# A fused LayerNorm, linear attention and MLP kernel: two of its four batches normalised with channels on the partitions

## The chip, the cores and the metric

The kernel runs on one core of a Trainium2 chip. The metric is the time of one execution on the device in microseconds (us); a kernel's time is the median of its runs. The engines are TensorE (PE; its weight loads are PEld), VectorE (DVE), ScalarE (ACT), GpSimd (POOL) and SyncE (SP), which here issues every DMA, in the order of its program.

## The reference

`x` has 4 batches of 512 tokens and 512 channels, in float32. Scales, shapes and names are shortened:

```python
xn = (x - mean(x)) / sqrt(var(x) + 1e-5)            # over the channels
q, k, v = xn @ wq.T, xn @ wk.T, xn @ wv.T           # 16 heads of 128; k and v have 4
o = lightning_attn(rope(q), rope(k), v)             # causal, decay exp(-lam_h * (i - j))
s = o @ wo.T
f = silu(xn @ fp8(gate_w) * gate_scale) * (xn @ fp8(up_w) * up_scale)   # 1536 wide
g = silu(f @ fp8(down_w) * down_scale)
out = x + s * g
```

## The kernel before

`xn` is used with channels on the partitions. Each product's operands are kept in two parts, a rounded one ("hi", a cast to fp32r by ScalarE) and the rest ("lo", a subtraction by VectorE or GpSimd). P = 128, KT = TT = 4 (channel tiles and token tiles), MT = 12 tiles of the hidden dimension. Batches are taken in `ORDER = [1, 2, 3, 0]`, and `s` is the position in it, so `s` = 2 and 3 are the third and fourth batch taken. A LayerNorm tile `i` is tile `i % 4` of batch `i // 4`.

*LayerNorm.* `load_x(i)` (L292) brings a tile of 128 tokens, tokens on the partitions, into one of 6 slots of `stage`. VectorE takes its statistics (`tile_stats`, `mean_var`, `inv_std`; the power runs on GpSimd). For `s` = 0 and 1 VectorE normalises, for `s` = 2 and 3 ScalarE (`norm`, L505). TensorE turns the tile with four transposes of 128x128 (`ln_transpose`, L1333) into a PSUM bank, ScalarE casts it to `xn`'s high part (`norm_hi`, L510), VectorE writes the rest (`norm_lo`, L809). Transposes of `s` = 2 and 3 all use bank 7.

*First loop (L1397), `m` = 0 to 11.* TensorE runs `gate_up` for `s` = 0 and 1 (each a gate and an up product chain of 8 matmuls), then `down(m - 2)` of `s` = 0; the engines beside it round the weights to fp8 values (`w_exponent`, `w_floor`, `w_round`). The tiles of `s` = 2 are turned at `m` = 7 to 10.

*Second loop (L1406), steps (`s`, `m`) with `s` = 2, then 3.* A step is `gate_up(s, m)`, for `m` < 4 a tile of `v` (`v_tile`, bank 7), then `down` of the batch before it. `gate_up` has three banks: `silu_gate(m)` (ScalarE) frees the gate's, which the up chain of `m` + 1 takes, and `fuse(m)` (VectorE) the up's, which the gate chain of `m` + 2 takes. `fuse_hi` (ScalarE) and `fuse_rest` (GpSimd) split `f` for `down`. At (2, 4) to (2, 7) the tiles of `s` = 3 are turned. In each step from (2, 1) to (3, 4) half a tile of `v` is multiplied by decay (`vd_mult`, VectorE), cast (`vd_round`, ScalarE), subtracted (`vd_rest`, VectorE) and stored as `v_decayed` (`store_vd`, SP); it has two buffers, so `vd_round` waits for the stores of the step before:

```python
if y >= 2:
    act.wait_ge(vd_out[y % 2], 16 * (y // 2))
```

At (3, 0) ScalarE makes the gates of `s` = 1 (`gates`, L546), for which TensorE waits before its first `down` of `s` = 2; ScalarE's `v_round` and VectorE's `v_rest` free bank 7 for the next `v_tile`. `spill_xn` and `spill_last` store `xn` (2 MB each batch, for `s` = 3 in four parts from (2, 8) on), and the first `attn_w` (1.28 MB) is loaded into `stage` at (2, 8).

*Attention.* After the second loop, 16 steps (head group, batch) follow, with `transpose_k` (L1440) in each. The change doesn't touch them.

The order on each engine is that of the program; engines meet through the semaphores named in the code.

## Time and profile before

| what | value |
|---|---|
| median of 3 runs | 905.67 us (905.59 to 906.05) |
| profiled execution, its time | 905.21 us |
| its span, first to last instruction | 903.4 us |
| TensorE busy | 895.4 us, 99% |
| VectorE busy | 632.6 us, 70% |
| ScalarE busy | 418.6 us, 46% |
| GpSimd busy | 373.4 us, 41% |
| DMA | 138.55 MB, mean 153 GB/s |

The span lies 1.8 us inside the time of its execution. The first loop ends near 147 us, the second near 312 us; the attention takes the rest. Busy shares are means over stages with different limits; busy time of TensorE is counted from the start of a matmul to its modelled end, so matmuls that follow one another overlap, and what one costs is read from the distance between starts.

### The profile page before, as it was taken

Reading aid. Unit: us, or ns where it says so; the run is one execution under the profiler, and the core shown is the slowest. Engines: PE = TensorE matmul, PEld = TensorE weight load, DVE = VectorE, ACT = ScalarE, POOL = GpSimd, SP = SyncE. Lnnn points to the kernel's source line nnn. Section 1 sums busy time; section 2 is a strip of 40 time slices with the busy share of each in tenths; the row PEclk is TensorE's granted clock in tenths of the full one; section 3 lists DMA queues with packets and bytes.
Section 4 is the critical chain, followed back from the end, with each engine's and each line's share of the span. In section 5 each row is a group of like instructions: output and inputs, shape, how many; then the busy total and the mean of one; then the engine's idle time right before and its main releaser. Section 6 shows DMA issues by size and latency. Waiting matters only on the chain.

```text
span 903.4 us, 12444 instructions
## 1 busy us (share of the span) xinstructions
PE 895.4 (99%) x4122; PEld 739.6 (82%) x4122; DVE 632.6 (70%) x905; ACT 418.6 (46%) x705; POOL 373.4 (41%) x276
## 2 busy tenths in 40 slices
PE   8999999999999999999999999999999999999997
PEld 5878888888888888888888888888888888888886
DVE  7978653677653257766777867677767677788797
ACT  3443533443433456444455444463554554634542
POOL 1011112122122475536555456365454563553547
PEclk9999999999999999999999999999999999999999
DMA  6792304379760624413333513244243043264482
GB/s 213 212 398 89 105 24 152 143 254 322 276 223 6 210 94 161 153 43 144 140 117 141 190 55 140 69 181 169 81 163 131 32 178 145 95 234 147 165 259 82
DMA packets 51115, 138.55 MB, mean 153 GB/s; under 512 B 4224, under 2 KB 25344, under 8 KB 45696
## 3 DMA queue, kind: packets, MB, share of 16 engines
q1 hardware_dynamic: 51072, 138.00, 43.2%
q8 instruction: 24, 0.39, 0.2%
q14 instruction: 19, 0.16, 0.1%
HBM read 96.04 MB, written 41.94 MB: 153 GB/s over the span
## 4 chain that ended last, share of the span: by engine, by line
PE 86%; issue 6%; POOL 4%; DVE 3%; ACT 1%; DMA 0%; POOLq 0%; SPq 0%; DVEq 0%; ACTq 0%
PE bank L1274 85%; POOL d_r L1210 2%; POOL rot L1219 1%; PE bank L1332 1%; PE bank L1294 0%; DMA stage<-in_x_nat 0%; DVE tail_sb L1116 0%; PE bank L1448 0%; DVE wst L834 0%; DVE d_sb L1019 0%; DVE tail_sb L1118 0%; ACT mag L522 0%; DVE tail_sb L1102 0%; DVE fz L851 0%; DVE acc L1112 0%
## 5 line engine op out<-in xcount | busy, mean ns | idle before, releaser
L1274 PE MATMUL bank<-xn,aw 128*128 128x512 f32 x960 | 229.1, 390 | 0.0
L1219 POOL TENSOR_TENSOR rot<-rot 128x512 f32<-128x512 f32 x80 | 126.9, 1586 | 234.9 <-DVE rot L1006 234.9
L1274 PEld LDWEIGHTS bank<-xn,aw 128*128 128x128 f32 x960 | 179.0, 188 | 37.3 <-issue 0.7
L1274 PE MATMUL bank<-o_r,ow 128*128 128x512 f32 (+1 forms) x792 | 186.2, 385 | 0.0
L1210 POOL TENSOR_TENSOR d_r<-d_sb,d_r 128x512 fp32r<-128x512 f32 x127 | 166.9, 1339 | 37.2 <-ACT d_r L692 37.1
L1274 PE MATMUL bank<-xn,gu_w 128*128 128x512 f32 x768 | 180.0, 389 | 0.4 <-DVE fz L851 0.4
L1274 PEld LDWEIGHTS bank<-xn,gu_w 128*128 128x128 f32 x768 | 144.1, 188 | 30.9 <-DVE dn_w L843 0.8
L1274 PEld LDWEIGHTS bank<-o_r,ow 128*128 128x128 f32 x792 | 144.4, 188 | 28.5
L1005 DVE TENSOR_TENSOR rot<-bank,rope 128x512 f32<-128x512 f32 x80 | 55.2, 690 | 102.6 <-ACT rot L672 102.5
L671 ACT COPY rot<-bank 64x512 f32<-64x512 f32 x80 | 46.8, 585 | 154.6 <-PE bank L1274 154.2
L692 ACT CAST d_r<-d_sb 128x512 fp32r<-128x512 f32 x128 | 79.0, 621 | 84.6 <-DVE d_sb L1065 62.2
L1191 POOL TENSOR_TENSOR fsplit<-f_all,fsplit 128x512 fp32r<-128x512 f32 x36 | 48.0, 1339 | 130.3 <-ACT fsplit L544 130.3
L1274 PE MATMUL bank<-fsplit,dn_w 128*128 128x512 f32 x384 | 94.7, 392 | 0.0
L1019 DVE TENSOR_TENSOR d_sb<-rot,q_decay 128x256 f32<-128x256 f32 x64 | 88.8, 1405 | 1.2 <-POOL rot L1219 1.2
L1274 PEld LDWEIGHTS bank<-fsplit,dn_w 128*128 128x128 f32 x384 | 71.3, 188 | 14.9 <-issue 0.3
L1065 DVE TENSOR_TENSOR d_sb<-bank,decay 128x512 f32<-128x512 f32 x96 | 64.2, 686 | 22.0 <-PE bank L1274 20.6
L1274 PE MATMUL bank<-q_r,k_r 128*128 128x512 f32 x288 | 78.2, 391 | 0.0
L1274 PE MATMUL bank<-d_r,v_r 128*128 128x512 f32 (+1 forms) x336 | 76.8, 361 | 0.4 <-POOL d_r L1210 0.4
L1274 PEld LDWEIGHTS bank<-d_r,v_r 128*128 128x128 f32 x336 | 57.5, 188 | 13.1 <-POOL d_r L1210 2.0
L1274 PEld LDWEIGHTS bank<-q_r,k_r 128*128 128x128 f32 x288 | 53.1, 188 | 10.3
L851 DVE SCALAR_TENSOR_TENSOR f_all<-bank,scale_sb,f_all 128x512 f32<-128x512 f32 x36 | 26.9, 748 | 47.0 <-PE bank L1274 36.7
L1191 POOL TENSOR_TENSOR fsplit<-fz,fsplit 128x512 fp32r<-128x512 f32 x12 | 15.5, 1294 | 103.3 <-ACT fsplit L544 103.3
(87 smaller groups left out, 973.4 us busy)
## 6 DMA issues: line engine op xcount, KB each, us to landing
xn<-xn_split SPq DMA_DIRECT2D x15, 2048.0 KB, 7.8
v_decayed<-vd_split SPq DMA_DIRECT2D x32, 512.0 KB, 3.5
vd_r<-v_decayed SPq DMA_DIRECT2D x16, 1024.0 KB, 7.2
v_r<-v_split SPq DMA_DIRECT2D x16, 512.0 KB, 5.8
wst<-in_mlp_w SPq DMA_DIRECT2D x10, 768.0 KB, 5.2
xn_split<-xn SPq DMA_DIRECT2D x3, 2048.0 KB, 10.7
stage<-in_attn_w SPq DMA_DIRECT2D x4, 1280.0 KB, 5.7
stage<-in_x_nat SPq DMA_DIRECT2D x16, 256.0 KB, 5.0
```

Source lines behind the costliest of these rows:

```text
L671: act.copy(rot2[0:ROT, r % RRING, :], ps[ROT:, :])
L692: act.copy(d_r[:, slot(e), 0, :], d_sb[:, slot(e), :]).then_inc(d_hi, 1)
L851: dve.scalar_tensor_tensor(out=f, in0=gu_ps[(2 * u + 1) % 3][:], scalar=scale_sb[:, MT + m:MT + m + 1], in1=f, op0=ALU.mult, op1=ALU.mult) ...
L1005: dve.tensor_tensor(rot1[:, r % RRING, :], proj_bank(n, r)[:], rope[:, 0, :], ALU.mult)
L1019: dve.tensor_tensor(d_sb[:, slot(e), bass.ts(h % 2, HALF)], rot1[:, (h + 1) % RRING, HALF:S], q_decay[:, h, :], ALU.mult).then_inc(q_decay ...
L1065: dve.tensor_tensor(by_head(d_sb[:, slot(e), :]), by_head(sc_ps[t % TRING][:]), decay[:, h0:h0 + nh, i0 - j:i0 - j + ni, :], ALU.mult).the ...
L1191: pool.tensor_tensor(fsplit[:, e % FRING, 1, :], src, fsplit[:, e % FRING, 0, :].bitcast(F32), ALU.subtract).then_inc(f_lo, 1)
L1210: pool.tensor_tensor(d_r[:, slot(e), 1, :], d_sb[:, slot(e), :], d_r[:, slot(e), 0, :].bitcast(F32), ALU.subtract).then_inc(d_lo, 1)
L1219: pool.tensor_tensor(rot1[:, r % RRING, :], rot1[:, r % RRING, :], rot2[:, r % RRING, :], ALU.add).then_inc(qk_sum, 1)
L1274: last = pe.matmul(dst, a, b, start=start and x == 0, stop=stop and x == len(pairs) - 1)
L1332: last = pe.transpose(ln_ps(i)[:, bass.ts(k, P)], stage[:, i % XRING, bass.ts(k, P)], ident[:])
```

## The change

For `s` = 0 and 1 nothing changes. For `s` = 2 and 3, x is still loaded with tokens on the partitions, for its statistics alone. Mean and rstd of the batch (128 partitions, 4 + 4 columns) are copied side by side into `row_in_sb`, turned by one transpose (`turn_rows`) into 8 partitions of 128, copied to `row_sb` (`row_round`), stored to DRAM (`store_rows`), and loaded from there as two rows of 512 tokens, each spread over all 128 partitions (`load_rows`), into the first half of `gout`. x is loaded again with channels on the partitions (`load_xt`, from `x_t`, which the kernel already has as an input). VectorE subtracts the one row and multiplies by the other (`norm_t`); ScalarE casts (`norm_t_hi`), VectorE writes the rest (`norm_t_lo`). The transposes of `ln_transpose` for tiles 8 to 15, ScalarE's `norm` and the `norm_hi` and `norm_lo` of those tiles are gone.

The places move: `norm_t` of `s` = 2 stands at `m` = 10 and 11 of the first loop, that of `s` = 3 at (2, 7) and (2, 8). `spill_last` and the load of `attn_w` go from (2, 8) to (2, 10) and on. The diff, without its declarations of semaphores and its blank lines:

```diff
 SPILL = 4
-LND = 4
+SPILL_AT = [(2, 10), (2, 11), (3, 0), (3, 1)]
+NAT = [i % XRING for i in range(3 * TT)] + [4, 5, 0, 1]
+TURNED = {2: [0, 1, 2, 3], 3: [2, 3, 4, 5]}
...
         xn_dram = nc.dram_tensor("xn_split", (NB, P, 2, KT, S), F32, kind="Internal").ap()
+        row_dram = nc.dram_tensor("ln_rows", (2, 2 * TT, P), F32, kind="Internal").ap()
...
         rstd = sb("rstd", [P, NB * TT], scope=mlp)
-        nmr = sb("nmr", [P, NB * TT], scope=mlp)
+        row_in_sb = sb("row_in_sb", [P, 2 * TT], scope=mlp)
+        row_sb = sb("row_sb", [2 * TT, P], scope=mlp)
         mlp.close()
+        rows = gout[:, 0:2, :]
...
...
-            return bank[i % TT] if i < 2 * TT else bank[7]
+            return bank[i % TT]
...
             def load_x(i):
-                if i >= XRING:
+                if i >= 3 * TT + 2:
+                    sp.wait_ge(ln_lo, 2 * TT + NAT[i] + 1)
+                elif i >= 3 * TT:
+                    sp.wait_ge(stats_d, i - 1)
+                elif i >= XRING:
                     sp.wait_ge(ln_t, i - XRING + 1)
-                sp.dma_start(stage[:, i % XRING, :], x_nat[ORDER[i // TT], :, i % TT, :]).then_inc(x_in[i % XRING], 16)
+                sp.dma_start(stage[:, NAT[i], :], x_nat[ORDER[i // TT], :, i % TT, :]).then_inc(x_in[NAT[i]], 16)
+            def store_rows(s):
+                sp.wait_ge(row_d, s - 1)
+                sp.dma_start(row_dram[s - 2], row_sb[:]).then_inc(row_out, 16)
+            def load_xt(s, k):
+                if s == 2:
+                    sp.wait_ge(ln_t if k < 2 else stats_d, 2 * TT if k < 2 else 2 * TT + k - 1)
+                else:
+                    sp.wait_ge(ln_lo if k < 2 else stats_d, 2 * TT + k + 3 if k < 2 else 3 * TT + k - 1)
+                sp.dma_start(stage[:, TURNED[s][k], :], x_t[k, :, bass.ts(ORDER[s], S)]).then_inc(xt_in[k], 16)
+            def load_rows(s):
+                if s == 2:
+                    for r in range(2):
+                        sp.wait_ge(v_out[r], 32 * (2 * TT // VFIRST))
+                else:
+                    sp.wait_ge(gate_out, 16 * KT)
+                sp.wait_ge(row_out, 16 * (s - 1))
+                for r in range(2):
+                    row = row_dram[s - 2, r * TT:(r + 1) * TT].rearrange("t p -> (t p)")
+                    sp.dma_start(rows[:, r, :], row.unsqueeze(0).broadcast_to([P, S])).then_inc(row_in, 16)
...
                 load_w(m)
+            store_rows(2)
+            for k in range(KT):
+                load_xt(2, k)
+            load_rows(2)
...
                         store_vd(*VD_AT[s, m])
+                    if s == 2 and m == 4:
+                        store_rows(3)
+                    if s == 2 and 2 <= m < 2 + KT:
+                        load_xt(3, m - 2)
+                    if s == 2 and m == 5:
+                        load_rows(3)
...
                         fetch_v((m + 1) // 2)
-                    if s == 2 and m >= MT - SPILL:
-                        spill_last(m - (MT - SPILL))
-                    if (s, m) == (2, MT - SPILL):
-                        sp.wait_ge(ln_t, NB * TT)
+                    if (s, m) in SPILL_AT:
+                        spill_last(SPILL_AT.index((s, m)))
+                    if (s, m) == SPILL_AT[0]:
+                        sp.wait_ge(ln_lo, NB * TT)
...
         def _(act):
-            def norm(i):
-                act.wait_ge(rstd_d, i // TT + 2)
-                act.activation(stage[:, i % XRING, :], stage[:, i % XRING, :], ACT.Identity,
-                               bias=nmr[:, i:i + 1], scale=rstd[:, i:i + 1]).then_inc(normed, 1)
...
                 act.wait_ge(ln_t, i + 1)
-                if i == 3 * TT:
-                    act.wait_ge(xn_out0, 16)
...
                          ln_ps(i)[:].rearrange("p (k c) -> p k c", k=KT)).then_inc(ln_hi, 1)
+            def row_round(s):
+                act.wait_ge(row_t, s - 1)
+                if s > 2:
+                    act.wait_ge(row_out, 16 * (s - 2))
+                act.copy(row_sb[:], bank[7][0:2 * TT, 0:P]).then_inc(row_d, 1)
+            def norm_t_hi(s, k):
+                act.wait_ge(scaled, (s - 2) * KT + k + 1)
+                if s == 3 and k == 0:
+                    act.wait_ge(xn_out0, 16)
+                    act.wait_ge(gu_done, 2 * UNIT[1, MT - 1] + 2)
+                act.copy(xn_of(s)[:, 0, k, :], stage[:, TURNED[s][k], :]).then_inc(ln_hi, 1)
...
                     w_floor(PARTS * SLABS + m + 2 - SLABS)
-                if m in (6, 7):
-                    norm(2 * TT + 2 * (m - 6))
-                    norm(2 * TT + 2 * (m - 6) + 1)
-                if 7 <= m < 7 + TT:
-                    norm_hi(2 * TT + m - 7)
+                if m == 7:
+                    row_round(2)
+                if m in (MT - 2, MT - 1):
+                    norm_t_hi(2, 2 * (m - MT + 2))
+                    norm_t_hi(2, 2 * (m - MT + 2) + 1)
...
                         v_round(VT_AT[s, m])
-                    if s == 2 and m in (2, 3):
-                        norm(3 * TT + 2 * (m - 2))
-                        norm(3 * TT + 2 * (m - 2) + 1)
-                    if s == 2 and LND <= m < LND + TT:
-                        norm_hi(3 * TT + m - LND)
+                    if s == 2 and m == 4:
+                        row_round(3)
+                    if s == 2 and m in (7, 8):
+                        norm_t_hi(3, 2 * (m - 7))
+                        norm_t_hi(3, 2 * (m - 7) + 1)
...
             def tile_stats(i):
-                dve.wait_ge(x_in[i % XRING], 16 * (i // XRING + 1))
-                dve.bn_stats(stats[:, i, :], stage[:, i % XRING, :]).then_inc(stats_d, 1)
+                dve.wait_ge(x_in[NAT[i]], 16 * (NAT[:i].count(NAT[i]) + 1))
+                dve.bn_stats(stats[:, i, :], stage[:, NAT[i], :]).then_inc(stats_d, 1)
...
                 dve.wait_ge(newton, c + 3)
-                dve.scalar_tensor_tensor(out=nmr[:, i0:i1], in0=mv[:, i0:i1, 0], scalar=-1.0, in1=rstd[:, i0:i1],
-                                         op0=ALU.mult, op1=ALU.mult).then_inc(rstd_d, 1)
+                if grp > 3:
+                    dve.wait_ge(row_t, grp - 3)
+                dve.tensor_copy(row_in_sb[:, 0:TT], mv[:, i0:i1, 0]).then_inc(row_src, 1)
+                dve.tensor_copy(row_in_sb[:, TT:2 * TT], rstd[:, i0:i1]).then_inc(row_src, 1)
...
                 dve.tensor_tensor(lo, ln_ps(i)[:].rearrange("p (k c) -> p k c", k=KT), hi.bitcast(F32),
+                                  ALU.subtract).then_inc(ln_lo, 1)
+            def norm_t(s, ks):
+                dve.wait_ge(row_in, 32 * (s - 1))
+                c = (s - 2) * KT
+                for k in ks:
+                    dve.wait_ge(xt_in[k], 16 * (s - 1))
+                    xt = stage[:, TURNED[s][k], :]
+                    dve.tensor_tensor(xt, xt, rows[:, 0, :], ALU.subtract).then_inc(centred, 1)
+                for k in ks:
+                    dve.wait_ge(centred, c + k + 1)
+                    xt = stage[:, TURNED[s][k], :]
+                    dve.tensor_tensor(xt, xt, rows[:, 1, :], ALU.mult).then_inc(scaled, 1)
+            def norm_t_lo(s, k):
+                dve.wait_ge(ln_hi, s * TT + k + 1)
+                dve.tensor_tensor(xn_of(s)[:, 1, k, :], stage[:, TURNED[s][k], :], xn_of(s)[:, 0, k, :].bitcast(F32),
...
                     inv_std(3)
-                if 7 <= m < 7 + TT:
-                    norm_lo(2 * TT + m - 7)
+                if m in (MT - 2, MT - 1):
+                    norm_t(2, (2 * (m - MT + 2), 2 * (m - MT + 2) + 1))
+                if m == MT - 1:
+                    norm_t_lo(2, 0)
+                    norm_t_lo(2, 1)
                 fuse(1, m)
+            norm_t_lo(2, 2)
+            norm_t_lo(2, 3)
...
                         v_rest(VT_AT[s, m])
-                    if s == 2 and LND <= m < LND + TT:
-                        norm_lo(3 * TT + m - LND)
+                    if s == 2 and m in (7, 8):
+                        norm_t(3, (2 * (m - 7), 2 * (m - 7) + 1))
+                    if s == 2 and m in (8, 9):
+                        norm_t_lo(3, 2 * (m - 8))
+                        norm_t_lo(3, 2 * (m - 8) + 1)
...
                     pe.wait_ge(ln_lo, v + TT)
+                    pe.wait_ge(v_lo, v)
...
                     pe.wait_ge(ln_lo, i - TT + 1)
-                elif i in (2 * TT, 3 * TT):
-                    pe.wait_ge(v_lo, i)
-                elif i > 2 * TT:
-                    pe.wait_ge(ln_lo, i)
...
                 last.then_inc(ln_t, 1)
+            def turn_rows(s):
+                pe.wait_ge(row_src, 2 * (s - 1))
+                pe.wait_ge(v_lo, TT if s == 2 else 3 * TT)
+                pe.transpose(bank[7][0:2 * TT, 0:P], row_in_sb[:], ident[:]).then_inc(row_t, 1)
...
                 gate_up(UNIT[1, m])
-                if 7 <= m < 7 + TT:
-                    ln_transpose(2 * TT + m - 7)
+                if m == 7:
+                    turn_rows(2)
...
                         v_tile(VT_AT[s, m])
-                    if s == 2 and LND <= m < LND + TT:
-                        ln_transpose(3 * TT + m - LND)
+                    if s == 2 and m == 4:
+                        turn_rows(3)
```

## Rows read from the trace of the kernel before

**Rows 1.** Page, parts 1 and 2: busy time, and the granted clock in 40 slices.
```profile
PE 895.4 (99%) x4122; PEld 739.6 (82%) x4122; DVE 632.6 (70%) x905; ACT 418.6 (46%) x705; POOL 373.4 (41%) x276
...
PEclk9999999999999999999999999999999999999999
```

**Rows 2.** Busy time by stretch: PE, PEld, DVE, ACT, POOL (instructions), clock, DMA share, GB/s.
```profile
60.00:147.00 87.00, 87.00 (x393) 71.97 (x392) 55.55 (x68) 34.10 (x44) 13.93 (x11) 1.00 0.30 115
147.00:312.00 165.00, 165.00 (x736) 136.38 (x735) 92.17 (x129) 72.06 (x122) 38.74 (x30) 1.00 0.58 205
```

**Rows 3.** Timeline, TensorE: start us, us from first start to last end, instructions.
```profile
94.38 1.98 PE L1274 MATMUL bank<-fsplit,dn_w 128*128 128x512 f32 x8
96.19 7.42 PE L1274 MATMUL bank<-xn,gu_w 128*128 128x512 f32 x32
103.45 0.60 PE L1332 MATMUL bank<-ident,stage 128*128 128x128 f32 x4
...
105.74 7.43 PE L1274 MATMUL bank<-xn,gu_w 128*128 128x512 f32 x32
...
183.40 0.60 PE L1332 MATMUL bank<-ident,stage 128*128 128x128 f32 x4
...
185.70 3.80 PE L1274 MATMUL bank<-xn,gu_w 128*128 128x512 f32 x16
```

**Rows 4.** Timeline, TensorE, first step of the attention part.
```profile
356.82 0.38 PE L1448 MATMUL bank<-ident,rot 128*128 128x128 f32 x2
...
359.79 2.88 PE L1274 MATMUL bank<-xn,aw 128*128 128x512 f32 x12
362.51 2.88 PE L1274 MATMUL bank<-o_r,ow 128*128 128x512 f32 x12
365.23 2.88 PE L1274 MATMUL bank<-xn,aw 128*128 128x512 f32 x12
```

**Rows 5.** Groups by line and form, 60 to 330 us: busy us, mean ns, idle before.
```profile
L886 DVE TENSOR_TENSOR vd_split<-vd_sb,vd_split 128x512 fp32r<-128x512 f32 x32 | 21.6, 688 | 21.9 <-ACT vd_split L582 21.6
L544 ACT CAST fsplit<-f_all 128x512 fp32r<-128x512 f32 x34 | 21.1, 622 | 6.7 <-PE bank L1274 6.6
...
L507 ACT ACTIVATE stage<-stage,nmr,rstd 128x512 f32<-128x512 f32 x8 | 6.1, 807 | 0.0
...
L813 DVE TENSOR_TENSOR xn<-bank,xn 128x512 fp32r<-128x512 f32 x8 | 5.5, 687 | 13.3 <-ACT xn L515 13.3
...
L515 ACT CAST xn<-bank 128x512 fp32r<-128x512 f32 x8 | 4.7, 581 | 1.7 <-PE bank L1332 1.6
```

**Rows 6.** Tile `v_decayed`, 150 to 260 us: landing times of its stores.
```profile
DMA to landing us min/median/max: 2.6/3.6/8.1
```

**Rows 7.** Timeline, VectorE (first row) and TensorE.
```profile
138.27 0.75 DVE L851 SCALAR_TENSOR_TENSOR fz<-bank,scale_sb,fz 128x512 f32<-128x512 f32 x1 [3.52 <-PE bank L1274]
...
147.13 3.79 PE L1274 MATMUL bank<-xn,gu_w 128*128 128x512 f32 x16
...
197.57 3.80 PE L1274 MATMUL bank<-xn,gu_w 128*128 128x512 f32 x16
...
225.28 3.79 PE L1274 MATMUL bank<-xn,gu_w 128*128 128x512 f32 x16
228.91 2.88 PE L1274 MATMUL bank<-wv,xn 128*128 128x512 f32 x12
231.63 1.98 PE L1274 MATMUL bank<-fsplit,dn_w 128*128 128x512 f32 x8
```

**Rows 8.** Timeline, GpSimd (first row) and VectorE.
```profile
188.42 1.30 POOL L1191 TENSOR_TENSOR fsplit<-f_all,fsplit 128x512 fp32r<-128x512 f32 x1 [6.38 <-ACT fsplit L544]
...
188.58 1.69 DVE L872 TENSOR_TENSOR v_raw<-vs 128x512 f32<-128x512 f32 x1
...
203.16 1.28 DVE L886 TENSOR_TENSOR vd_split<-vd_sb,vd_split 128x512 fp32r<-128x512 f32 x2
```

**Rows 9.** Timeline, ScalarE, the gates of the batch `s` = 1.
```profile
228.64 2.42 ACT L551 ACTIVATE gout<-bank,scale_sb 128x512 f32<-128x512 f32 x4
```

More of the change, by code:

```diff
@@ L228, in attention_mlp_kernel @@
         floor_c = sem("floor_c"); newton = sem("newton"); rstd_d = sem("rstd_d")
+        row_src = sem("row_src"); row_t = sem("row_t"); row_d = sem("row_d"); row_out = sem("row_out"); row_in = sem("row_in"); xt_in = [sem(f"xt_in{k}") for k in range(KT)]; centred = sem("centred"); scaled = sem("scaled")
         normed = sem("normed"); ln_t = sem("ln_t"); ln_hi = sem("ln_hi"); ln_lo = sem("ln_lo")
```

## The prediction

> **What bounds the kernel now.** I read the page first: what is busy, and at what clock. TensorE is busy 99% of the span and the granted clock is in its highest tenth in every slice, the level of 2.4 GHz [rows 1]. Then the busy time by stretch, for the two stretches that the change touches: from 60 to 147 us (`s` = 0 and 1 side by side) and from 147 to 312 us (`s` = 2 and then 3) TensorE is busy for all of both, and VectorE for 64% and 56% [rows 2]. So nobody makes TensorE wait there: each instruction that it no longer executes shortens the kernel by its pitch, unless another engine then comes late. Last I read the timelines: TensorE's for the pitch, VectorE's, ScalarE's and the queue's for how late they already are.
>
> **What is removed.** 32 transposes in 8 groups of 4, each after a `gate_up` and before a `down`. A profile's duration of a pipelined matmul is not its price; the distance between starts is. Without a group, the 8 products of `down` take from 94.38 to 96.19, 1.81 us. With a group, the distance from the transposes to the next `gate_up` is 105.74 - 103.45 = 2.29 us, and in the later stage 185.70 - 183.40 = 2.30 us [rows 3]. So a group costs 0.48 to 0.49 us, and 8 cost 3.9 us.
>
> The Trainium skill (TensorE: Matmul & The Clock Gate, section "Part 4: PE-mode transpose") gives about 275 ns for a transpose in a kernel's context. By that the 32 would be worth 8.8 us, an estimate. A transpose of four lasts 0.27 us in this trace too (0.60 us for four that start 0.12 us apart), but I go by the starts.
>
> **What is added on TensorE.** Two transposes of `row_in_sb` (128x8). The nearest row is the pair in `transpose_k`: with it, 12 products take 359.79 - 356.82 = 2.97 us, without it 365.23 - 362.51 = 2.72 us [rows 4], so 0.12 us each if it is linear, 0.25 us each if the pair's price is all fixed, and nothing at best. I take 0.12, the price per piece that the groups of four show too (0.49 / 4): 0.25 us for both, bounds 0 and 0.5.
>
> Net: 905.21 - 3.9 + 0.25 = 901.56 us for the profiled execution. Its time is 0.46 us below the median of the runs, 905.67; against that median the sum is 902.0.
>
> **What moves to other engines.** ScalarE loses 8 normalisations of 0.80 us and 8 casts of 0.58 us, and gets 8 casts of 0.62 us and two tiny ones: it gains time. VectorE loses 8 subtractions from PSUM of 0.69 us, and gets 24 operations on SBUF of 0.69 us, one every 0.60 us (the pair at 203.16 takes 1.28) [rows 5, 8]: about 9.6 us more in all. In total VectorE's idle time covers that [rows 2]. What decides is where it stands. The queue gets 8 loads of `x_t` (256 KB each), 4 spread rows of 256 KB and 2 tiny stores: some 3 MB.
>
> *The batch `s` = 2, prepared at `m` = 10, 11 of the first loop.* The row path starts at `turn_rows(2)` after `gate_up(1, 7)`, near 103.5 us; even with a store and a load at 8.1 us each, the longest landing of stores of `v_decayed` [rows 6], the rows are there by about 121, and `norm_t` runs only after `fuse(0, 10)`, at 129. Behind those waits on SP stand only loads of x. The hand-over to `gate_up(2, 0)`: `fuse(0, 11)` began at 138.27 [rows 7]; 0.67 for it, 2.4 for four passes, 1.2 for two subtractions, 0.67 for `fuse(1, 11)`, 1.3 for the last two: 144.6, or 145.9 if the GpSimd subtraction stands in the way once (1.3 us). `gate_up(2, 0)` started at 147.13 [rows 7]; all of this shifts together. Covered by 1.2 to 2.5 us, so costed at nothing; with the cover gone, `gate_up(2, 0)` waits for the difference. `spill_xn(2)` (2 MB) now waits for these last subtractions; behind it on SP stand the stores of the gates, which wait for `down(11)` anyway. The x tiles 14 and 15 wait for the first two `norm_t_lo` and are read at (2, 1), more than a unit later.
>
> *GpSimd in the way.* When `v_raw` was added at 188.58, with GpSimd's subtraction running from 188.42, it took 1.69 us [rows 8], where a subtraction of the same shape takes 0.69 [rows 5]. Each of the new passes has two SBUF operands too, so each can be held for up to 1.3 us; `norm_lo` read PSUM. The Trainium skill (SBUF — State Buffer, section "SBUF: two separate sides") says that VectorE with two SBUF inputs and GpSimd exclude each other for a whole instruction; the trace agrees, 1.69 against 0.69 us. It is the rule that speaks against this change. I count one collision below, where ScalarE's release of GpSimd falls on VectorE's start.
>
> *The batch `s` = 3, prepared at (2, 7) to (2, 9), which is `gate_up`'s (`s`, `m`).* Here VectorE is already full: `vd_mult`, `fuse`, `vd_rest`. I write it out from the start of `gate_up(2, 7)` (197.57 before) as 0. A unit is 3.63 + 1.81 = 5.44 us [rows 3, 7], so the starts are 5.44, 10.88, 16.3, 21.8, and 27.2 for (3, 0).
> - (2, 7): the last `vd_rest` ends at 6.9, as before (203.16 + 1.28) [rows 8]. Two centrings, two scalings: 9.3. ScalarE waits for them and casts to 9.9.
> - (2, 8): ScalarE's `fuse_hi` and `silu_gate` end at 11.1; `up(2, 9)` needs them at 12.7. VectorE: `fuse` 11.8, `vd_rest` 13.0, `norm_t` 15.5, two `norm_t_lo` 16.7.
> - (2, 9): ScalarE's gate is done at 17.3, needed at 18.1. VectorE's `v_raw` collides with GpSimd, 18.6; products 19.8, `fuse` 20.5, needed at 21.8; `vd_rest` 21.7, the last two `norm_t_lo` 22.9.
> - (2, 10), (2, 11): `vd_round` waits for the stores of `v_decayed` before it (landing 2.6 to 8.1, median 3.6 us [rows 6]). With 3.0 us it is done with (2, 11) at 30.8, with 3.6 us at 31.9. Then the four gates, 2.42 us [rows 9]: 33.2 to 34.3. `down(3, 0)` needs them at 27.2 + 3.63 + 2.72 = 33.55. Before, they ended at 228.64 + 2.42 = 231.06 and were needed at 231.63 [rows 7, 9]: the margin was 0.57 us already. So 0 to 0.75 us of stall.
> - (3, 0): ScalarE's `vd_round` waits for stores issued at 31.0 to 31.8, now behind `spill_last` and the 1.28 MB of `attn_w` (moved from `m` = 8 to `m` = 10). `v_round(12)` and `v_rest(12)` stand behind it, and `v_tile(13)` wants the bank at 27.2 + 8.16 + 3.63 = 39.0. With a landing of 3.6 us the bank is free by about 37.8 to 38.4, with 5.2 us at 39.6, with 8.1 at 42.5: 0 to 3.5 us.
>
> For the two places together I take 0.5 us, nearer the lower end, as the median landing is 3.6; bounds 0 and 4.2. ScalarE's gain at `m` = 2 to 7 speaks for the lower end. The other new waits (`row_out` at `load_rows(3)`, behind which on SP stand the stores of `m` = 6; `turn_rows(3)` on `v_lo`, which the first transpose of `s` = 3 waited for before too) are met units ahead: nothing.
>
> **Forecast:** 902.0 + 0.5 = 902.5 us, faster by 0.35%.
>
> **Rivals.**
> - *A. The slack at (2, 10) to (3, 1) is gone:* a stall of 1.8 to 5.4 us that eats half to all and more of the gain, time 903.9 to 907.5, likeliest near 904.5. For it: margins of 0.8, 1.3 and 0.57 us, and the landing of 8.1 us. Against it: the transfers that made that landing leave `m` = 8.
> - *B. Slower:* one mechanism, stores of `v_decayed` late behind the spill and `attn_w` at (2, 11), so `v_tile(13)` waits for its bank. Above 907.5 it needs a stall of 5.5 us, so a landing of 10 to 11 us after an issue at 31.8: longer than any landing in that row. Say 12 us: 46.4 - 39.0 = 7.4 us, 909.4.
> - *C. TensorE's transposes were worth nothing or much more.* Worth nothing would be 905.9; TensorE has no idle time in which they could hide [rows 2]. Worth their duration of 0.27 us instead of 0.12, the time would be near 897; the starts speak against it [rows 3].
>
> **How the numbers follow.** A measurement of this kernel tells about 0.2%, 1.8 us, from no change. The forecast with a stall of 0 to 1.8 us has 0.70; A 0.17 within the bound and 0.01 of it beyond; B 0.08; C 0.02 for the nothing and 0.02 for the much. Faster: 0.72. Same: 0.19. Slower: 0.09. The forecast's own range is 901.5 (added transposes free, 0.25 us for noise) to 903.8. The range of 8 in 10 takes in A to 905.5, where under 0.2 is left out on top and below: 901.3 to 905.5.
>
> **What would show it.** Between `down(e)`'s first product and the next `gate_up`, 1.81 us everywhere but after the two `turn_rows` (about 1.95). TensorE still without idle time to (2, 11); if it stalls, at `down(3, 0)` for a gate, at `v_tile(13)` for `v_lo`, or at `up(2, 10)`. VectorE's passes at 0.69 us, some near 1.7. ScalarE idle some 2.5 us at (2, 7) before its casts. Wrong, if the row transposes cost more than 0.3 us, if the spread loads of one DRAM row land after 10 us or more, which no row shows, or if the landing of the stores at (2, 10) doubles.

## The result, and the profile after

The changed kernel takes 908.63 us (median of 8 runs, 907.91 to 910.32) against 905.64 us (8 runs, 905.46 to 906.38): the ratio is 1.0034, 95% interval 1.0025 to 1.0043. It is slower by 3.0 us, where 902.5 us was forecast.

In the profiled execution (span 906.7 us, against 903.4) TensorE executes less, and is busy less, as against [rows 1]:

```profile
PE 892.9 (98%) x4092; PEld 737.1 (81%) x4092; DVE 646.1 (71%) x923; ACT 413.6 (46%) x699; POOL 374.3 (41%) x276
```

The waits of TensorE, in the changed kernel (us in total, times, longest):

```profile
PE bank L1411 <- DVE stage L861: 2.4, 1, 2.4
PE bank L1356 <- ACT gout L604: 1.5, 1, 1.5
PE bank L1356 <- ACT f_all L588: 1.5, 2, 1.0
...
PE bank L1356 <- DVE vs L935: 1.3, 1, 1.3
```

Before, TensorE was busy for all of the stretch from 147 to 312 us [rows 2]. Now it waits there four times for the banks of `gate_up` (1.03 and 0.48 us), for the gates (1.53) and for the bank of `v_tile` (1.32). The timeline of TensorE shows where, and what each really costs:

```profile
182.80 0.27 PE L1418 MATMUL bank<-ident,row_in_sb 128*8 128x128 f32 x1
182.83 2.09 PE L1356 MATMUL bank<-fsplit,dn_w 128*128 128x512 f32 x8
...
206.51 1.98 PE L1356 MATMUL bank<-xn,gu_w 128*128 128x512 f32 x8
209.52 2.11 PE L1356 MATMUL bank<-xn,gu_w 128*128 128x512 f32 x8 [1.03 <-ACT f_all L588]
211.47 1.98 PE L1356 MATMUL bank<-fsplit,dn_w 128*128 128x512 f32 x8
213.28 1.98 PE L1356 MATMUL bank<-xn,gu_w 128*128 128x512 f32 x8
215.74 2.11 PE L1356 MATMUL bank<-xn,gu_w 128*128 128x512 f32 x8 [0.48 <-ACT f_all L588]
217.69 1.98 PE L1356 MATMUL bank<-fsplit,dn_w 128*128 128x512 f32 x8
...
228.57 2.88 PE L1356 MATMUL bank<-wv,xn 128*128 128x512 f32 x12
232.98 2.08 PE L1356 MATMUL bank<-fsplit,dn_w 128*128 128x512 f32 x8 [1.53 <-ACT gout L604]
234.90 3.79 PE L1356 MATMUL bank<-xn,gu_w 128*128 128x512 f32 x16
240.00 3.06 PE L1356 MATMUL bank<-wv,xn 128*128 128x512 f32 x12 [1.32 <-DVE vs L935]
242.90 1.98 PE L1356 MATMUL bank<-fsplit,dn_w 128*128 128x512 f32 x8
```

Read the distances between starts, as in [rows 3, 7]. A transpose of the rows costs 182.80 to 184.75, the start of the next `gate_up`, less 1.81: 0.14 us. The first loop, from the same `down` at 95.62 (94.38 before) to `gate_up(2, 0)` at 146.53 (147.13), is 1.84 us shorter than before, which is what four groups less and one small transpose more should give. Then `gate_up(2, 9)` (from 206.51) takes 4.96 us for 3.63, `gate_up(2, 10)` (from 213.28) 4.41 for 3.63, `v_tile(12)` with its wait 4.41 for 2.72, `gate_up(3, 1)` with the wait behind it 5.10 for 3.63; with the slower restarts (0.11 and 0.18) that is 5.6 us lost, some 0.3 us more at each place than the wait itself. Gained and lost: -3.9 + 0.3 + 5.6 = +2.0 us of the 3.3 by which the spans differ.

The first two of these stalls come from `silu_gate(2, 8)` and `silu_gate(2, 9)`, each of which frees the bank that the up chain of the next step takes. The expectations below name the stalls after these gates, (2, 8) and (2, 9); TensorE stands in `gate_up` of (2, 9) and (2, 10).

Nearly all of the rest is at the start. The stretches of the page's window view at 8 to 12 us (PE, PEld, DVE, ACT, POOL, clock, DMA share, GB/s) show the clock at its lower level, after TensorE had stood idle for 2.36 us before its first transpose:

```profile
8.00:10.00 2.00, 1.26 (x6) 1.29 (x7) 1.89 (x7) 0.76 (x2) 0.00 (x0) 0.60 1.04 376
10.00:12.00 2.00, 2.00 (x9) 1.10 (x7) 1.54 (x6) 2.00 (x5) 0.70 (x1) 0.55 0.63 234
```

That is 1.2 us by `down` at 95.62; the first transpose itself starts 0.57 us late (8.74 for 8.17), and the rest follows at the lower clock. The code there is unchanged, and later profiles of kernels with the change had the same place within 0.5 us of before, so it belongs to this execution. The medians differ by 3.0 us all the same, so that other executions lose about 1 us at some place that this profile doesn't show.

### The profile page after: what moved, and what is told of

It is laid out like the page before. It is cut to its first block, busy times and chain, and to the rows that moved or that the text cites. A ratio compares the mean times of both kernels' runs of the same rounds, so it can differ in the third digit from the quotient of the medians.

```text
span 906.7 us, 12414 instructions
## 1 busy us (share of the span) xinstructions
PE 892.9 (98%) x4092; PEld 737.1 (81%) x4092; DVE 646.1 (71%) x923; ACT 413.6 (46%) x699; POOL 374.3 (41%) x276
## 4 chain that ended last, share of the span: by engine, by line
PE 79%; issue 6%; DVE 5%; POOL 4%; DMA 3%; ACT 1%; SPq 1%; POOLq 0%; DVEq 0%; ACTq 0%
PE bank L1356 78%; POOL d_r L1292 2%; DMA v_decayed<-vd_split 2%; POOL rot L1301 1%; DMA vs<-v_split 1%; DVE vd_split L960 1%; DMA stage<-in_x_nat 0%; PE bank L1376 0%; DVE tail_sb L1198 0%; PE bank L1533 0%; DVE wst L908 0%; DVE d_sb L1101 0%; DVE tail_sb L1200 0%; PE bank L1411 0%; DVE f_all L925 0%
## 5 line engine op out<-in xcount | busy, mean ns | idle before, releaser
L713 ACT CAST q_r<-rot 128x512 fp32r<-128x512 f32 x64 | 39.8, 622 | 39.2 <-POOL rot L1301 38.4
```

The costliest lines, as they stand in the source:

```text
L713: act.copy(dst, rot1[:, r % RRING, :]).then_inc(qk_hi, 1)
```

## Why TensorE waits: the transfers first

SyncE's timeline at (2, 5) and VectorE's at (2, 7), changed kernel:

```profile
192.67 0.46 SPq L318 DMA_DIRECT2D stage<-in_x_t  x1
193.23 1.16 SPq L330 DMA_DIRECT2D gout<-ln_rows  x2
194.43 0.98 SPq L379 DMA_DIRECT2D vs<-v_split  x2
195.67 9.99 SPq L386 DMA_DIRECT2D v_decayed<-vd_split  x4
...
201.41 0.69 DVE L946 TENSOR_TENSOR v_raw<-vs 128x512 f32<-128x512 f32 x1 [4.58 <-DMA vs<-v_split]
...
205.22 1.28 DVE L878 TENSOR_TENSOR stage<-stage,gout 128x512 f32<-128x512 f32 x2
...
195.63 3.79 PE L1356 MATMUL bank<-xn,gu_w 128*128 128x512 f32 x16
```

The last row is TensorE's `gate_up(2, 7)`. The fetch of v stands behind a tile of `x_t` and the two spread rows. VectorE is idle for 4.58 us until it lands, and `norm_t` starts at 205.22, 9.6 us after `gate_up(2, 7)` (195.63), not 6.9. So the first theory (T) was: the fetch is late, and all else follows. Its rivals were VectorE's added passes (R1) and the spill and `attn_w` at (2, 10) (R2).

### The first four experiments

**e1: the fetch ahead of the new loads.**
```diff
+                    if s == 2 and m in (3, 5, 7, 9):
+                        fetch_v((m + 1) // 2)
                     if s == 2 and 2 <= m < 2 + KT:
                         load_xt(3, m - 2)
                     if s == 2 and m == 5:
                         load_rows(3)
-                    if s == 2 and m in (3, 5, 7, 9):
-                        fetch_v((m + 1) // 2)
```


> The changed kernel, but at (2, 3) and (2, 5) the fetch of v is issued before the loads of x_t and of the spread rows. Theory T (the fetch of v at (2, 5) stands behind the spread rows on SP's queue, lands at 201.4, and VectorE waits 4.6 us for it at (2, 7)): that wait is gone or under 1.5 us, the stalls of TensorE at (2, 8) and (2, 9) are gone, those at (3, 0) and (3, 1) shrink; 903.5 to 905.5 us. Rival R1 (VectorE's added passes at (2, 7), (2, 8) are too much by themselves): the stalls stay above 3 us in all, 907.5 us or more. Rival R2 (the loss is made by the spill and attn_w moved to (2, 10)): the stalls at (3, 0) and (3, 1) stay at 3.2 us, 906.5 to 907.5 us.

908.56 us against 905.59, ratio 1.0040 (1.0026 to 1.0053). The theory in that form is wrong. VectorE no longer waits for the fetch (0.22 us at (2, 7)), but the next transfer on the queue, the stores of `v_decayed`, is late in its place, and ScalarE waits for it. ScalarE and SyncE in e1:

```profile
201.98 0.62 ACT L635 CAST vd_split<-vd_sb 128x512 fp32r<-128x512 f32 x1 [4.57 <-DMA v_decayed<-vd_split]
...
194.21 0.84 SPq L330 DMA_DIRECT2D gout<-ln_rows  x2
195.14 9.79 SPq L386 DMA_DIRECT2D v_decayed<-vd_split  x4
```

`norm_t` starts at 204.49, 9.8 us after `gate_up(2, 7)`: nothing won. The time alone would fit R1, but the idle time is still that of a transfer. TensorE loses 2.3 us at (2, 9) and (2, 10) and 4.3 at (3, 0) and (3, 1).

**e2: without the spread rows of `s` = 3.**
```diff
-                    if s == 2 and m == 5:
-                        load_rows(3)
...
-                dve.wait_ge(row_in, 32 * (s - 1))
+                dve.wait_ge(row_in, 32)
+                if s == 3:
+                    dve.wait_ge(gate_d, KT)
```


> The changed kernel without the load of the spread rows for s = 3; its norm_t takes what lies in gout, so that the fourth batch's numbers are not the reference's. T: the fetch of v lands early, as if it stood first, 903.5 to 905.5 us. R1: same stalls as in the changed kernel, 908 us. R2: 906.5 to 907.5 us.

907.49 us (905.70 to 909.83) against 905.59, ratio 1.0019 (1.0009 to 1.0028): by the median R2's range. In the profile, of the 905.70 us run, TensorE loses under 0.1 us at (2, 9) and (2, 10), but still 3.8 at (3, 0) and (3, 1). So the loads at (2, 5) make the first two stalls, and something else makes the other two.

**e3: the same bytes, not spread.**
```diff
-                    sp.dma_start(rows[:, r, :], row.unsqueeze(0).broadcast_to([P, S])).then_inc(row_in, 16)
+                    src = row.unsqueeze(0).broadcast_to([P, S]) if s == 2 else x_t[r, :, 0:S]
+                    sp.dma_start(rows[:, r, :], src).then_inc(row_in, 16)
```


> The changed kernel, but the two loads for s = 3 read the same 512 KB from x_t without spreading (the fourth batch is normalised with wrong rows). If reading one 2 KB row of DRAM 128 times is what is slow: the fetch of v behind them lands some 2 us earlier and the time falls by 2 us or more, to 906.5 us or less. If it is the place in the queue and the bytes: within 0.7 us of the changed kernel, 908 to 909 us. R1 and R2: 908 to 909 us.

908.81 us against 905.59, ratio 1.0039 (1.0026 to 1.0053), 0.2 us from the changed kernel. That one row of DRAM is read 128 times is not what is slow; the place and the bytes are left, and this run doesn't tell them apart.

**e4: the spill and `attn_w` later.**
```diff
-SPILL_AT = [(2, 10), (2, 11), (3, 0), (3, 1)]
+SPILL_AT = [(3, 1), (3, 2), (3, 3), (3, 4)]
```


> The changed kernel, with spill_last and the load of attn_w moved from (2, 10) on to (3, 1) on. R2: stalls at (3, 0) and (3, 1), 3.2 us, are gone, 905 to 906 us. T: the stall at (3, 0) (1.7 us) stays, as it follows from vd_round being late since (2, 7); the one at (3, 1) shrinks: 907 to 908.5 us. R1: as T.

905.98 us (904.69 to 908.89) against 905.59, ratio 1.0007 (0.9997 to 1.0016): 2.65 us won against the changed kernel, a time in R2's range. In the profile the wait at `v_tile(13)` is gone, those at (2, 9), (2, 10) (1.29 and 0.49 us) and at (3, 0) (1.20) stay. R2 expected the one at (3, 0) gone too: it is right for one of the four waits. The stores of (2, 11), for which ScalarE waits at (3, 0), landed in 6.7 to 7.0 us in the changed kernel and in 2.7 to 2.9 here.

### Both places, one half, and the loads alone

**e5: loads apart and spill late**, and **e6: loads apart, spill as in the change.** Both:
```diff
+                    if s == 2 and m in (3, 5, 7, 9):
+                        fetch_v((m + 1) // 2)
-                    if s == 2 and 2 <= m < 2 + KT:
-                        load_xt(3, m - 2)
-                    if s == 2 and m == 5:
+                    if s == 2 and 1 <= m < 1 + KT:
+                        load_xt(3, m - 1)
+                    if s == 2 and m == 6:
                         load_rows(3)
-                    if s == 2 and m in (3, 5, 7, 9):
-                        fetch_v((m + 1) // 2)
```
and e5 with e4's line as well.

> The changed kernel with x_t for s = 3 loaded one step earlier, at (2, 1) to (2, 4), the spread rows at (2, 6), each behind that step's fetch of v, and the spill and attn_w from (3, 1) on. Theory T2 (what is late is whatever transfer stands behind 0.75 MB of added loads at (2, 5): the fetch of v in the changed kernel, the stores of v_decayed in e1; the passes of VectorE alone fit): no stall of TensorE at (2, 8) and (2, 9) over 0.3 us in all, none at (3, 1); 902.0 to 903.8 us. R1 (VectorE's passes are too much by themselves): stalls at (2, 8), (2, 9) of 1.5 us or more stay, 905.5 us or more, as e4.

> As e5, but the spill and attn_w from (2, 10) on, as in the changed kernel. T2 with both causes separate (loads at (2, 5), spill at (2, 10)): stalls only at (3, 0) and (3, 1), 1 to 3 us; 904 to 906.5 us. If the stalls at (3, 0) and (3, 1) are only the lateness of (2, 7) carried on: 902.0 to 903.8 us, as e5. R1: 908 us.

e5: 904.28 us against 905.55, ratio 0.9990 (0.9981 to 0.9999). e6: 909.28 us (906.42 to 910.74), ratio 1.0039 (1.0025 to 1.0053). e5 lies 0.5 us above T2's range; e6 is 2.8 us above it, and 1.3 above R1's figure. Yet in both, the last `vd_rest` of (2, 7) ends 7.0 us after `gate_up(2, 7)`, as the prediction had it, and of the 2.1 us that TensorE lost at (2, 9) and (2, 10), 0.3 us are left in e5 and 0.5 in e6. In e6 `v_tile(13)` then waits 2.55 us, and that costs more than the wait. TensorE in e6:

```profile
238.34 4.59 PE L1356 MATMUL bank<-wv,xn 128*128 128x512 f32 x12 [2.55 <-DVE vs L935]
242.76 1.98 PE L1356 MATMUL bank<-fsplit,dn_w 128*128 128x512 f32 x8
```

And the windows of e6 (columns as above):

```profile
238.00:240.00 2.00, 1.66 (x4) 1.33 (x5) 1.93 (x3) 0.55 (x1) 1.27 (x1) 0.64 0.55 178
240.00:242.00 2.00, 2.00 (x6) 1.56 (x5) 1.85 (x3) 0.00 (x0) 0.00 (x0) 0.51 1.10 397
242.00:244.00 2.00, 2.00 (x10) 1.65 (x10) 0.25 (x1) 0.62 (x1) 0.00 (x0) 1.00 1.04 424
```

After the idle time the granted clock is 0.64 and 0.51 for some 4 us, and the 12 products take 4.42 us in place of 2.72. The wait costs 2.7 us and the clock 1.7, so that e6's time says nothing for R1. The one run of e6 whose mean granted clock was 0.999 took 906.42 us, the five at 0.995 to 0.997 took 908.34 to 910.74.

**e7: the change for `s` = 2 alone.** `s` = 3 is normalised, turned and spilled as before the change. Of its diff:
```diff
-SPILL_AT = [(2, 10), (2, 11), (3, 0), (3, 1)]
+SPILL_AT = [(2, 8), (2, 9), (2, 10), (2, 11)]
...
-                    if s == 2 and m == 4:
-                        turn_rows(3)
+                    if s == 2 and LND <= m < LND + TT:
+                        ln_transpose(3 * TT + m - LND)
```


> The change for s = 2 alone; s = 3 is normalised as in the kernel before, with the spill and attn_w at (2, 8) to (2, 11). All theories: four groups of transposes less (1.94 us), one transpose of rows more (0.14 us), no new stall: 903.6 to 904.3 us. If the third batch's part has a cost of its own (hand-over to gate_up(2, 0), the later 2 MB spill): 905 us or more.

904.16 us (903.23 to 905.10) against 905.55, ratio 0.9981 (0.9972 to 0.9989). Half the change keeps its gain, 1.4 us of the 1.8 worked out; its profile has one wait of 0.24 us in the second loop and none there besides. The path by way of DRAM, the passes of VectorE and the later 2 MB spill cost nothing for `s` = 2 that the interval, 0.8 us either way, could tell.

**e8: the kernel before, with the loads alone.** 1.5 MB that nobody uses, at the change's places (the diff without its waits; the gates of `s` = 1 and the load of `attn_w` wait for these loads too, which had landed long before):
```diff
+                    if s == 2 and 2 <= m < 2 + KT:
...
+                        sp.dma_start(stage[:, 4 + m % 2, :], x_t[m - 2, :, bass.ts(0, S)]).then_inc(extra_in[m % 2], 16)
+                    if s == 2 and m == 5:
+                        sp.wait_ge(gate_out, 16 * KT)
+                        for r in range(2):
+                            sp.dma_start(gout[:, r, :], x_t[r, :, 0:S]).then_inc(extra_rows, 16)
                     if s == 2 and m in (3, 5, 7, 9):
                         fetch_v((m + 1) // 2)
```


> The kernel before, with as many bytes loaded and not used at the same places of SP's queue: 256 KB of x_t at (2, 2) to (2, 5) and 512 KB more at (2, 5). T2: VectorE or ScalarE waits 1 to 4 us longer at (2, 6), (2, 7) for a transfer, but nobody calls on the time, as norm_t isn't there: TensorE stalls 0 to 1 us, 905.6 to 906.8 us. If the loads alone make the loss: 908 us or more. If the transfers don't matter: 905.6 us and no longer waits.

907.87 us (907.17 to 908.26) against 905.55, ratio 1.0023 (1.0014 to 1.0031). T2 expected at most 1.2 us more than before, the case "the loads alone make the loss" 2.4 or more; it is 2.3. So the loads alone cost 2.3 us. That is most of the 3.0 us by which the changed kernel is slower, but about a third of the 6.6 us by which it misses the sum without stalls (902.0). VectorE, ScalarE and TensorE in e8:

```profile
203.74 0.69 DVE L886 TENSOR_TENSOR v_raw<-vs 128x512 f32<-128x512 f32 x1 [3.81 <-DMA vs<-v_split]
...
224.89 0.62 ACT L596 CAST vd_split<-vd_sb 128x512 fp32r<-128x512 f32 x1 [6.43 <-DMA v_decayed<-vd_split]
...
231.37 2.42 ACT L565 ACTIVATE gout<-bank,scale_sb 128x512 f32<-128x512 f32 x4
...
229.50 2.89 PE L1288 MATMUL bank<-wv,xn 128*128 128x512 f32 x12
233.93 2.08 PE L1288 MATMUL bank<-fsplit,dn_w 128*128 128x512 f32 x8 [1.54 <-ACT gout L565]
```

VectorE waits 3.8 us for the fetch at (2, 7), 28 us before TensorE waits. TensorE loses nothing there, nor at (2, 9) and (2, 10); the lateness is carried along. ScalarE waits 6.4 us for a store at (2, 10), where it waited 4.8 before, and the gates start at 231.37 for 228.64, 2.7 us late, where the margin was 0.57 us [rows 7, 9]. With 0.3 us in `gate_up(3, 0)` and a slower restart, the 1.54 us wait costs 2.1. No pass of VectorE and no transpose has been touched in this kernel.

**e11: the same loads at e5's places.** Against e8:
```diff
-                    if s == 2 and 2 <= m < 2 + KT:
+                    if s == 2 and m in (3, 5, 7, 9):
+                        fetch_v((m + 1) // 2)
+                    if s == 2 and 1 <= m < 1 + KT:
...
-                    if s == 2 and m == 5:
+                    if s == 2 and m == 6:
...
-                    if s == 2 and m in (3, 5, 7, 9):
-                        fetch_v((m + 1) // 2)
```


> The kernel before with the same 1.5 MB of unused loads as in e8, but at e5's places: x_t at (2, 1) to (2, 4), 512 KB at (2, 6), each behind the fetch of v. T2 (the place counts): e8's stall of 1.5 us at (3, 0) is under 0.5 us, 905.5 to 906.3 us. If the bytes count wherever they stand: 907.5 us or more, as e8.

905.91 us against 905.56, ratio 1.0003 (0.9994 to 1.0012). The same bytes one step off and behind the fetch cost nothing that is measured; TensorE waits 0.76 us once, at the transposes of (2, 6), and not at the gates. T2 holds in this: the place counts.

One question stays open. The DMA engines are busy without a break from 192 to 196 and from 198 to 202 us in the changed kernel (DMA share 1.03 and more in each 2 us). All these loads are issued by SyncE, and no run issues them from another queue, so the order on the queue and the full DMA engines aren't told apart.

### What is left in e5: the passes, and the order on ScalarE

In e5 `down(3, 0)` still waits for the gates. VectorE (two products of `vd_mult`, two subtractions of `norm_t_lo`), ScalarE and TensorE:

```profile
212.95 2.26 DVE L952 TENSOR_TENSOR vd_sb<-v_raw,k_decay 128x512 f32<-128x512 f32 x2
...
217.00 2.38 DVE L887 TENSOR_TENSOR xn<-stage,xn 128x512 fp32r<-128x512 f32 x2
...
225.07 0.62 ACT L635 CAST vd_split<-vd_sb 128x512 fp32r<-128x512 f32 x1 [2.10 <-DVE vd_sb L952]
227.10 0.62 ACT L635 CAST vd_split<-vd_sb 128x512 fp32r<-128x512 f32 x1 [1.41 <-DMA v_decayed<-vd_split]
227.62 2.41 ACT L604 ACTIVATE gout<-bank,scale_sb 128x512 f32<-128x512 f32 x4
...
222.15 3.79 PE L1356 MATMUL bank<-xn,gu_w 128*128 128x512 f32 x16
...
230.18 2.06 PE L1356 MATMUL bank<-fsplit,dn_w 128*128 128x512 f32 x8 [1.53 <-ACT gout L604]
```

Two operations of VectorE that take 1.28 us take 2.26 and 2.38 when GpSimd works beside them (its subtractions run from 212.37 for 1.70 us and from 216.47 for 1.76). `vd_round` of (2, 11) ends at 227.7 and the gates at 230.0; TensorE wanted them at 222.15 + 6.35 = 228.5.

**e9: e5 without the centring and scaling of `s` = 3**; the fourth batch goes in unnormalised. ScalarE's casts then wait for the loads of `x_t` in place of the scaling:
```diff
-                act.wait_ge(scaled, (s - 2) * KT + k + 1)
+                if s == 2:
+                    act.wait_ge(scaled, k + 1)
+                else:
+                    act.wait_ge(xt_in[k], 32)
...
                 dve.wait_ge(row_in, 32 * (s - 1))
+                if s == 3:
+                    return
```


> e5 (loads apart, spill late) without VectorE's centring and scaling for s = 3; the casts and subtractions stay, so the fourth batch goes in unnormalised. In e5 TensorE still stalls 1.5 us at (3, 0) for the gates, and VectorE is never idle from (2, 7) to (2, 11). V (VectorE's 8 passes make that): the stall is gone, 902.0 to 902.8 us. L (what is left is still the transfers): the stall stays above 1 us, 903.8 us or more.

902.05 us against 905.56, ratio 0.9963 (0.9949 to 0.9976), and TensorE doesn't wait in the second loop. So VectorE's 8 passes, with ScalarE's waits for them, make what is left in e5: R1 in part, 2.2 us of it, on top of the transfers. In e5 ScalarE stands idle for 3.36 and 2.87 us until the scaled tiles are there, in e9 not at all; e9 doesn't tell VectorE's own time from these waits. (The expectation has VectorE never idle in e5 from (2, 7) to (2, 11); it is idle twice, 0.7 us each.)

**e10: e5 with the gates ahead of the casts.**
```diff
-                    if m == 0:
-                        gates(s - 2)
+                    if (s, m) == (2, 0):
+                        gates(0)
                     fuse_hi((s - 1) * MT + m + 1)
                     silu_gate(s, m)
+                    if (s, m) == (2, MT - 1):
+                        gates(1)
```


> e5 with ScalarE's gates of s = 1 put ahead of its vd_round of (2, 11), in place of after it. If the gates are late only because they stand behind casts that wait for VectorE and for stores: no stall at (3, 0), 902.0 to 903.0 us. If the delay is passed on to the casts and comes out at v_tile(13): a stall at (3, 1) of 0.5 us or more, 903 to 904.5 us.

902.70 us (902.14 to 903.91) against 905.56, ratio 0.9972 (0.9962 to 0.9983): the fastest kernel here that does all of the work, 2.9 us below the kernel before and 5.9 below the changed one. ScalarE in e10:

```profile
223.01 2.42 ACT L604 ACTIVATE gout<-bank,scale_sb 128x512 f32<-128x512 f32 x4
...
227.24 0.62 ACT L635 CAST vd_split<-vd_sb 128x512 fp32r<-128x512 f32 x1 [1.30 <-DMA v_decayed<-vd_split]
```

The gates are made from 223.0 on, ahead of the two casts of `vd_round`; the second of these still ends at 227.9, since it waits for a store and not for ScalarE.

**e12: the changed kernel with e10's move alone.** The diff is the one shown at e10.

> The changed kernel with e10's move of the gates alone: loads at (2, 5) and the spill at (2, 10) as in the change. If three causes stand one behind the other (loads at (2, 5) for the stalls at (2, 8), (2, 9), 2.1 us; gates behind the casts for (3, 0), 1.8 us; the spill for (3, 1), 1.6 us or more): the stall at (3, 0) is gone and the other two stay, 906.0 to 907.5 us. If the gates' place is all that matters: 904.5 us or less. If lateness is only handed on to v_tile(13): 908 us or more.

910.44 us against 905.52, ratio 1.0055 (1.0041 to 1.0069): worse than the changed kernel. The stall at (3, 0) is gone and reappears, larger, at `v_tile(13)`. SyncE, ScalarE, TensorE:

```profile
225.24 0.46 SPq L348 DMA_DIRECT2D xn_split<-xn  x1
225.74 1.11 SPq L442 DMA_DIRECT2D stage<-in_attn_w  x1
229.14 2.20 SPq L386 DMA_DIRECT2D v_decayed<-vd_split  x2
...
237.27 0.62 ACT L635 CAST vd_split<-vd_sb 128x512 fp32r<-128x512 f32 x1 [5.91 <-DMA v_decayed<-vd_split]
...
240.49 4.54 PE L1358 MATMUL bank<-wv,xn 128*128 128x512 f32 x12 [4.23 <-DVE vs L937]
244.87 1.98 PE L1358 MATMUL bank<-fsplit,dn_w 128*128 128x512 f32 x8
```

The stores of (2, 11) are issued from 229.14, behind 0.5 MB of spill and 1.28 MB of `attn_w`, and ScalarE waits for them until 237.27; 12 products then take 4.38 us, again at the lower clock (0.60 and 0.55 granted from 240 to 244 us). With the spill where it is, the wait at (3, 0) took the place of part of this one.

## Why the prediction was wrong, step by step

- *What is removed and added: right.* 0.48 us for each group of four, and 0.14 us for each transpose of rows (0.12 forecast, bounds 0 and 0.25): -3.6 us. e9 (902.05, without eight of VectorE's passes) has it whole, 3.5 us below the kernel before, e10 (902.70) nearly. Rival C is out. The Trainium skill (TensorE: Matmul & The Clock Gate, section "Part 4: PE-mode transpose") gives about 275 ns for a transpose in a kernel's context. As a duration the trace agrees with it (0.27 us); as a price it would make the 32 worth 8.8 us, an estimate, and the runs don't bear that out.
- *The batch `s` = 2: right.* Covered, as costed at nothing; e7.
- *"The queue gets 8 loads of `x_t` ..., 4 spread rows ...: some 3 MB": the step that failed.* They were counted and given no price. At (2, 5) three loads of 0.75 MB in all stand in front of a fetch (the changed kernel) or of stores (e1) that VectorE or ScalarE waits for at (2, 7). "(2, 7): the last `vd_rest` ends at 6.9, as before" was 9.7 in the changed kernel, and 7.0 in e5, where the loads stand elsewhere. That the new waits "are met units ahead: nothing" looked at who waits for the new transfers, and not at what stands behind them. The price is 2.3 us in e8, in the kernel before; in the changed kernel with its spill late, moving the loads wins 1.7 us (e4 to e5). The stalls at (2, 9) and (2, 10), 2.1 us for nothing in the forecast, need the loads and VectorE's passes together: e8 has the loads without the passes and no stall there, e5 the passes without the loads in that place and 0.3 us.
- *(3, 0), with the spill and `attn_w` at (2, 10): in the range, and above the 0.5 us taken for both places.* 0 to 3.5 us were given and rival B's mechanism named. It is 1.3 us of wait in the changed kernel, 2.6 in e6 and 4.2 in e12, and each of the last two costs 1.7 us more through the clock. The stores of (2, 11) were to be issued 31.0 to 31.8 us after `gate_up(2, 7)` and to land in 3.6; the changed kernel issues them from 34.1 us on (229.73 - 195.63), and they land in 6.7 to 7.0. Before, they landed in 2.6 to 3.0. So the prediction's own sign of being wrong, a landing that doubles, came one step later than it was looked for.
- *Rival B: its time came, its mechanism hardly.* The time is above its 907.5 us, but the bank of `v_tile(13)` makes 1.6 of the 5.6 us lost, and three other stalls the rest; that the sum lies where B had it is luck. That such a time needs a landing of 10 us was wrong too: in e12 landings of 7.4 to 8.1 us make a wait of 4.2, some 6 with the restart and the lower clock, since the stores are issued late already.
- *(2, 7) to (2, 11), VectorE's passes: right in kind, too small.* "I count one collision" with GpSimd; e5's VectorE has three that cost about 1 us each, between (2, 9) and (2, 11) (at 212.95, 217.00 and 222.66). That agrees with the exclusion of GpSimd and VectorE that the Trainium skill states (SBUF — State Buffer, section "SBUF: two separate sides"): 2.26 and 2.38 us where the same pairs take 1.28 alone. In e5's clean case the gates end 7.9 us after `gate_up(3, 0)` starts (230.03 - 222.15), where 6.0 to 7.1 was forecast and 6.35 needed: a stall of 1.5 us for 0 to 0.75.
- *What was not in the sum at all:* after the stalls of 1.83 us in e3, 2.55 in e6 and 4.23 in e12 the granted clock fell, which cost 1.6 to 1.7 us each time; after 2.77 us in e1 it didn't. The changed kernel's runs lie 2.4 us apart, those of the kernel before, measured beside it, 0.9. The mean granted clock of each run goes with its time: e4's six runs at 0.999 and 1.000 took 904.69 to 906.09 us, its four at 0.996 to 0.998 took 906.05 to 908.89. At which stall the clock fell in them, only a profile would show.

The causes are separate but not additive. From the changed kernel, by medians (the kernel before had 905.52 to 905.64 each time it was measured): spill late alone -2.65 us (e4), loads apart alone +0.65 (e6), both -4.35 (e5), gates first alone +1.8 (e12), all three -5.9 (e10). In e6 and e12 part of this is the lower clock.

## What to carry to other kernels

- A load costs what stands behind it on its queue (or on the same DMA engines, which these runs don't tell apart). For each DMA that a change adds, look at the next transfer on that queue and who waits for it, not only at who waits for the new one; move it one step, or behind the urgent one.
- A stage without idle time on TensorE can still be late: read how much margin each hand-over has (here 0.57 us at the gates) before loading the engines beside it. Lateness travels: in e8 VectorE's 3.8 us of waiting at (2, 7) came out 28 us later, as a wait of TensorE of 1.5 us.
- When stalls follow one another, taking one away can show the next. A fix that measures nothing or worse alone (e6, e12) may be needed in the end (e10).

## What the runs showed of the hardware

- Four loads of 256 KB in the changed kernel, each spreading one 2 KB row of DRAM over 128 partitions, landed in 4.5 to 5.9 us. Two plain loads of the same size in place of the last two landed in 5.8 to 5.9 and changed the time by 0.2 us (e3).
- The stores of (2, 11), 512 KB each, landed in 6.2 to 8.1 us when they were issued behind 0.5 MB of spill and 1.28 MB of `attn_w` (the changed kernel, e1, e2, e3, e6, e12), and in 2.6 to 3.3 where these transfers came later (e4, e5, e9, e10).
- TensorE's clock fell to its level of 1.2 GHz after some idle times and not after others. It fell after 2.36 us before the first transposes in the changed kernel (0.60 and 0.55 granted from 8 to 12 us), but not after 2.34 us at the same place in e3. It fell after 1.83 us at (3, 0) in e3, where 8 products of `down` took 3.40 us for 1.81, but not after 1.53 us there in the changed kernel, nor after 2.77 us at (3, 1) in e1. TensorE in e3 and e1:

```profile
232.67 3.60 PE L1357 MATMUL bank<-fsplit,dn_w 128*128 128x512 f32 x8 [1.83 <-ACT gout L605]
...
240.13 3.02 PE L1356 MATMUL bank<-wv,xn 128*128 128x512 f32 x12 [2.77 <-DVE vs L935]
```
